# Nearly equal column pieces for keys, queries and perceptron features, and 2-byte edge tables

## What is computed

```python
x = _layernorm(x + _L0_gnn_ref(x, src, dst, edge_type_8, edge_weight, ...))    # two relational convolutions, 4 bases
x = _layernorm(x + _L1_gnn_ref(x, bases, w_comp, h_bias, edge_weight1, ...))   # one relational convolution, 8 bases
x = _layernorm(x + _L2_gnn_ref(x, src, dst, deg, W1, b1, W2, b2))              # mean of neighbours
x = _layernorm(x + _L3_gnn_ref(x, edge_index, node_vec1, ...))                 # 4 attention blocks
# one block of L3, with 4 heads of 128 features
y = cond_layer_norm(x)
q, k, v = y @ wq + bq, y @ wk + bk, y @ wv + bv
x = x + softmax_over_edges(q[src] . k[dst]) v[dst] @ wo + bo
y = cond_layer_norm(x)
x = x + relu(y @ m_w1 + m_b1) @ m_w2 + m_b2
```

## Time and profile before

| what | value |
|---|---|
| device time, median of 3 runs | 3153.47 us (3148.95 to 3154.17) |
| span of the profiled execution | 3143.3 us |
| TensorE busy | 2966.4 us, 94% |
| VectorE busy | 2076.1 us, 66% |
| ScalarE busy | 1275.2 us, 41% |
| GpSimd busy | 1178.9 us, 38% |

### The profile page before, as it was taken

How to read it: one execution, slowest core, us unless ns; L and a number is a source line. 1 busy time by engine, 2 the same in 40 slices (tenths; PEclk the granted TensorE clock), 3 DMA queues, 4 the chain that set the end, 5 groups by cost and what they waited for, 6 DMA issues and landing times.

```text
span 3143.3 us, 42911 instructions
## 1 busy us (share of the span) xinstructions
PE 2966.4 (94%) x14658; PEld 2176.8 (69%) x14658; DVE 2076.1 (66%) x5081; ACT 1275.2 (41%) x2245; POOL 1178.9 (38%) x938
## 2 busy tenths in 40 slices
PE   5898998999979899999999999999999999999999
PEld 2333774445843357875458998889987999879987
DVE  7999224886358763444376677567766776767677
ACT  4666431002340033342254554355543555435554
POOL 4666336664456643432022123511135102431022
PEclk8999999999989999999999999999999999999999
DMA  2555524664246542333012001310113001130012
GB/s 80 166 168 161 166 96 136 171 173 143 81 131 179 169 124 89 95 99 121 12 45 88 15 31 50 101 43 8 37 57 118 14 8 65 44 104 15 8 64 80
DMA packets 129593, 279.31 MB, mean 89 GB/s; under 512 B 22742, under 2 KB 45590, under 8 KB 128354
## 3 DMA queue, kind: packets, MB, share of 16 engines
q0 software_dynamic: 40320, 132.15, 14.8%
q1 hardware_dynamic: 87618, 141.76, 14.2%
q10 hardware_dynamic: 1440, 2.62, 0.2%
HBM read 227.85 MB, written 27.48 MB: 81 GB/s over the span
## 4 chain that ended last, share of the span: by engine, by line
PE 74%; DVE 13%; another core or an unknown queue 6%; ACT 3%; issue 2%; DMA 2%; POOL 1%; DVEq 0%; SPq 0%; POOLq 0%; ACTq 0%
PE bank L155 16%; PE bank L157 16%; PE bank L156 16%; PE bank L889 9%; PE bank L2545 5%; PE bank L2209 3%; PE bank L1849 2%; PE bank L860 2%; DVE G L996 2%; DVE onehot_dst L963 1%; DVE y_tile L2161 1%; DVE y_tile L2163 1%; DVE x_stats L2144 1%; DMA yT_lo<-yT_new_lo 1%
## 5 line engine op out<-in xcount | busy, mean ns | idle before, releaser
L889 PE MATMUL bank<-gathered,selector 128*128 x1328 | 641.5, 606 | 57.7 <-SPq L848 30.9
L996 DVE TENSOR_TENSOR G<-G,bank 128x512 f32 x664 | 450.4, 678 | 23.5 <-PE bank L889 23.3
L889 PEld LDWEIGHTS bank<-gathered,selector 128*128 128x128 f32 x1328 | 231.8, 192 | 303.8 <-issue 167.2
L2633 ACT CAST probT<-bank 128x512 fp32r<-128x512 f32 (+2 forms) x480 | 212.2, 515 | 263.0 <-PE bank L2545 262.1
L1510 POOL TENSOR_TENSOR weight_parts<-weight_ring,weight_parts 128x512 fp32r<-128x512 f32 x130 | 188.0, 1446 | 296.7 <-ACT weight_parts L1443 296.6
L2715 DVE CUSTOM_DVE_ANT_0 prob<-bank,count_by_src 128x512 f32<-128x512 f32 (+1 forms) x480 | 258.4, 589 | 58.8 <-PE bank L157 58.8
L1469 DVE TENSOR_TENSOR lhs_parts<-G,lhs_parts 128x640 fp32r<-128x640 f32 x122 | 102.3, 840 | 288.4 <-ACT lhs_parts L1441 288.2
L2641 DVE TENSOR_TENSOR probT<-bank,probT 128x512 fp32r<-128x512 f32 (+2 forms) x480 | 254.0, 585 | 52.1 <-ACT probT L2633 51.3
L870 ACT COPY G<-bank 128x512 f32<-128x512 f32 x160 | 82.3, 654 | 492.2 <-remote 405.2
L155 PE MATMUL bank<-weight_parts,lhs_parts 128*128 128x512 f32 x680 | 268.7, 395 | 11.3 <-POOL weight_parts L1510 5.5
L157 PE MATMUL bank<-weight_parts,lhs_parts 128*128 128x512 f32 x680 | 266.5, 392 | 0.0
(11 more groups left out here) (295 smaller groups left out, 6807.5 us busy)
## 6 DMA issues: line engine op xcount, KB each, us to landing
weight_ring<-in_L_gnn_basis SPq DMA_DIRECT2D x64, 256.0 KB, 2.7
weight_ring<-in_L_gnn_bases SPq DMA_DIRECT2D x64, 256.0 KB, 2.7
x_L<-x_rows SPq DMA_DIRECT2D x50, 256.0 KB, 4.4
x_rows<-x_L SPq DMA_DIRECT2D x50, 256.0 KB, 5.8
yT_hi<-yT_new_hi SPq DMA_DIRECT2D x4, 2560.0 KB, 11.4
yT_lo<-yT_new_lo SPq DMA_DIRECT2D x4, 2560.0 KB
count_rows<-count SPq DMA_DIRECT2D x10, 642.0 KB, 5.7
count_by_dst<-count_rows SPq DMA_DIRECT2D x10, 642.0 KB, 4.6
```

Source lines behind the costliest of these rows:

```text
L889: ins = pe.matmul(bank[s % banks][:], sel[:, s % SELECTORS, :], tile_rows_of[s % BATCH], start=True, stop=True)
L996: ins = dve.tensor_tensor(g, g, bank[s % banks][:], ALU.add)
L2633: ins = act.copy(hi, of)
```

## The change

The pieces of `SPANS` become 432, 432 and 416 columns, those of `SEEN` 416, 416 and 418. The two waits that counted tiles of 512 columns follow. `tile_of_step`, `steps_of_tile` and the intermediate `tile_int` are held as 16-bit unsigned numbers in place of 32-bit ones; `window_of_step` stays 32-bit.

```diff
-F32, I32, BF16, F16 = mybir.dt.float32, mybir.dt.int32, mybir.dt.bfloat16, mybir.dt.float16
+F32, I32, U16, BF16, F16 = mybir.dt.float32, mybir.dt.int32, mybir.dt.uint16, mybir.dt.bfloat16, mybir.dt.float16
...
-SPANS = [(c, min(512, NP - c)) for c in range(0, NP, 512)]
+WIDE = [432, 416]
+SPANS = [(0, WIDE[0]), (WIDE[0], WIDE[0]), (2 * WIDE[0], NP - 2 * WIDE[0])]
...
-SEEN = [(c, min(512, N - c)) for c in range(0, N, 512)]
+SEEN = [(0, WIDE[1]), (WIDE[1], WIDE[1]), (2 * WIDE[1], N - 2 * WIDE[1])]
...
-    C.tile_of_step = {PATH1: M.new("tile_of_step", [1, PATH1.steps // BATCH, 2, BATCH], I32)}
-    C.steps_of_tile = {PATH1: M.new("steps_of_tile", [1, T], I32)}
+    C.tile_of_step = {PATH1: M.new("tile_of_step", [1, PATH1.steps // BATCH, 2, BATCH], U16)}
+    C.steps_of_tile = {PATH1: M.new("steps_of_tile", [1, T], U16)}
...
-    C.tile_of_step[PATH0] = M.new("tile_of_step", [1, PATH0.steps // BATCH, 2, BATCH], I32)
-    C.steps_of_tile[PATH0] = M.new("steps_of_tile", [1, T], I32)
+    C.tile_of_step[PATH0] = M.new("tile_of_step", [1, PATH0.steps // BATCH, 2, BATCH], U16)
+    C.steps_of_tile[PATH0] = M.new("steps_of_tile", [1, T], U16)
...
-    tile_i = M.new("tile_int", [1, PATH1.steps], I32)
+    tile_i = M.new("tile_int", [1, PATH1.steps], U16)
...
-            act.wait_ge(*relued(HID * i + KC * (j // 4 + 1)))
+            m = next(m for m, (c, width) in enumerate(SEEN) if min((j + 1) * P, N) <= c + width)
+            act.wait_ge(*relued(HID * i + KC * (m + 1)))
...
-                    pe.wait_ge(*y_lo(g + min(4 * m + 4, NT)))
+                    pe.wait_ge(*y_lo(g + -(-(c + width) // P)))
```

## The result

The changed kernel takes 3184.13 us (median of 5, 3181.37 to 3187.85) against 3153.47 us (median of 5 by now, 3148.95 to 3161.01): a ratio of 1.0098, 95% interval 1.0086 to 1.0110, so 31 us slower. Its profiled execution spans 3182.1 us.

What follows compares the result with a forecast made beforehand. TensorE, busy 94% of the 3143.3 us span, was taken as the bound. Tables +34, pieces -5 and new stall +6 gave +35 us; with 10.2 us around the span, 3188.5 us, range 3150 to 3212.

Steps and rivals of the forecast that it cites:

- the 10.2 us: Whole kernel: time taken to lie around the profiled span of 3143.3 us, against the timed median of 3153.47 us.
- The load: Edge-stage register loads: four 2-byte entries fetched entry by entry, 0.90 us in place of 0.329 us.
- The edge stages: Three edge stages: longer loads in the matmul queue leave 15 + 8 + 11 = 34 us after idle time.
- the raw 77 us: Edge stages: ceiling of matmul delay from longer loads, 26 + 15 + 36 us, before later waits take some up.
- The fourth rival: Edge stages: loads cost 0.90 us but idle time absorbs less, between 34 and 77 us; within the 0.63 forecast case.
- the 0.3 us in hand: Matmul queue at an edge-stage batch: about 0.3 us of slack, so 1.14 us more leaves 0.85 us bare.
- GpSimd at zero: GpSimd's 40 loads a stage grow by 0.57 us each but run ahead of the gathers: 0, or 23 us uncovered.
- The pieces' columns: Key projections, scores and perceptron: equal pieces save about 8 ns per narrow matmul, 5 us taken between 0 and 7.
- The new stall: Attention layer: score matmuls wait for the larger last key piece, 15 x 0.42 = 6.3 us, bounds 0 and 10.
- the third rival: Tables free and pieces gain in full because the last key piece is ready in time: 3146.5 us, chance 0.07.
- The perceptron's pieces at zero: Perceptron: its waits for tiles and features cost nothing; without cover, under 2 us, four times.
- The rival that the loads are free: Register loads: 2-byte loads cost the same 0.33 us as 4-byte ones, leaving +1 us, 3154.5 us; chance 0.25.

Runs made afterwards that it cites:

- tables: The kernel before with both tables in 2-byte entries and its column pieces unchanged: 3179.95 us, ratio 1.0086.
- split: The kernel before with 2-byte tables, next batch's slots loaded after its second step and tiles after the fourth: 3099.03 us against 3090.85, ratio 1.0026.
- GpSimd twice: The kernel before with 2-byte tables and each GpSimd load of steps_of_tile made twice: 3136.44 us, ratio 1.0146.
- asserted last 256: The kernel before with 4-byte tables, bounds tested on chip, keys and features in pieces of 512, 482, 256 columns: 3188.08 us, ratio 1.0107.

## Why the prediction was right, point by point

**The total.** 3188.5 us forecast, 3184.13 measured, slower by more than can be told from no change, inside the range. That it is this near is in part luck: two errors cancel. The added time between the profiled executions is 38.8 us, not 35. And the 10.2 us are not time around a span: the profiled execution of after took 3183.51 us with a span of 3182.1, so some 1.4 us lie there. The other 8.8 us are what the profiled execution of before was quicker than the median run. (Its device time is not on record; 3143.3 + 1.4 = 3144.7 us is below every timed run of before on these chips, the lowest of which took 3148.95 us.) After's was 0.6 us below its median. So the reading of "span plus 10.2" is wrong, and the medians moved by 31 us where the two executions moved by 39.

Part of that quickness goes with the granted clock. It was 0.988 in the profiled execution of before, and 0.985 to 0.987 in the nine runs of before that stood beside "tables": the four at 0.987 spanned 3148.6 to 3151.3 us, the two at 0.985 3153.5 and 3156.7 us. After had 0.987 to 0.989 in its five. The differences of stages below are taken against that quick execution and may be too large by some of the 8.8 us; in which stages, no run shows.

**The load: 0.90 us forecast, 0.985 us measured.** Mechanism right, term 9% small. I took the step from two entries (529 ns) against four (342 ns), but four are already the cheap case. The base is one entry at about 0.3 us and the step 0.22 us, which gives 0.3 + 3 x 0.22 = 0.96 us. The stop grew by 2.32 - 1.02 = 1.30 us a batch, not 1.14.

**The edge stages: 15 + 8 + 11 = 34 us forecast, 19.0 + 11.7 + 6.8 = 37.5 us measured.** Right in kind in the first two stages: TensorE's waits for issue grow by 24.9 and 9.2 us there, and about half of the raw 77 us is taken up in all. That these two were put low fits the longer stop. The third was put too high, and its loss has another look: the waits for issue grow by 3.0 of the 6.8 us, while TensorE's busy time grows by 5.8 us (259.4 to 265.2), with a granted clock of 0.99 before and 0.97 after from the stage's first to its last matmul on gathered rows. No run takes that apart. The fourth rival (less is absorbed) did not happen. That the lump and not the sum costs was in the prediction as the 0.3 us in hand; "split" shows it.

**GpSimd at zero.** Supported, not shown: TensorE's waits for gathers are 32.4 us in after, 31.9 us before, but "GpSimd twice" came out dearer than that account has room for.

**The pieces' columns: -5 us forecast, -2.6 us found.** This term was put about twice too large. Between "tables" and after, the score blocks lose 0.5 us, apart from the new stall, the projections of queries and keys 2.0 us and the perceptron's matmuls 0.1 us (from start to start, waits taken out). The 8 ns for each narrow matmul hold for the projections (64 x 3 of them, 1.5 us); of the 160 x 3 in the scores and the 64 x 3 in the perceptron, which should have given 5.4 us, only 0.6 us is found. The prediction's other bound, that a whole score block already ran at the proportional rate, was the better reading there.

**The new stall: 15 x 0.42 = 6.3 us forecast, 15 times and 5.3 us measured.** Place, count and cause are as forecast; ScalarE's 0.61 and VectorE's 0.65 us came out as interpolated, the piece was free to be read 1.83 us behind the start of the last projection matmul, not 1.75, and TensorE got there at 1.48 us, not 1.33. "asserted last 256" shows the cause: with a last piece of 256 columns the wait is gone. So the third rival (full gain) is refuted.

**The perceptron's pieces at zero.** This step failed, by 2.9 us. I looked at the products' own waits for tiles. What came late is the turning of the next normed tile (3.8 us in 8 waits, 0.9 in 3 before). In 7 of the 8, what stands between that turn and the one before it is one output slice, 12 matmuls, of 416 columns where it was 512. So TensorE is back 2.5 us after the earlier turn began, where it was 3.1 us before (both without the wait itself), and the tile's norm is not earlier. With a first piece of 512 columns ("asserted last 256") the wait is 1.2 us. The attention layer's sum is thus -2.6 + 5.3 + 2.9 = 5.6 us, near the 5.3 us by which it grew between the traces of "tables" and after, where I had +1. (TensorE's waits for the DMA of `yT_lo`, 3.1 us in "tables" and 1.2 in after, are not in it.)

**The rival that the loads are free** (0.25) fell with the first row of loads.

## What to carry to other kernels

Read tables for registers as 4-byte entries in aligned groups of four; a narrower type saves nothing but SBUF and triples the load. What a queue does between matmuls is free as long as each stop is shorter than the matmuls already handed over (here stops of 1.0 us cost nothing that could be told, of up to 1.25 us about 8 us in all, of 2.3 us 27 us): try to cut a long stop in two before making it cheaper. When columns are moved from wide pieces to the last one, look who takes that piece out of PSUM and who waits for it; here the smallest piece last did without both new waits of the equal pieces, though its gain over before could not be told from none.

## What the runs showed of the hardware

A register load took 0.28 to 0.33 us for one entry and 0.21 to 0.22 us more for each further one, for entries of 1, 2 and 4 bytes alike, on VectorE's and on GpSimd's queue. Four 4-byte entries that fill an aligned 16-byte group took 0.33 to 0.36 us together, eight 0.57 to 0.60 us, and the same four out of alignment 0.95 to 0.97 us. On the matmul queue four 4-byte entries took 0.33 us, four 2-byte entries 0.99 us and eight 1.92 us. Tests of a register's bounds were dearer than expected: a batch with four of them held the matmul queue for 2.16 us with loads of 0.33 us, and single queue operations lasted 0.7 us in the second and third stage.
